# Attention scores on one Trainium2 core: row maxima carried in a spare contraction row of masked queries, instead of in a pass of selector matmuls

## The reference: what is computed

```
patches -> h = patches @ W_embed + b_embed + pos          # 64 images, 196 rows of 256
h = concat(h, txt)                                        # 228 rows per image
q, k, v = LN(h) @ Wq.T, LN(h) @ Wk.T, LN(h) @ Wv.T        # 16 heads of 16
probs = softmax(causal(q k^T / 4));  ctx = probs @ v
h = h + ctx @ Wo.T + bo
h = h + FFN(LN(h))     # ternary weights, RMS norm before each linear, exact gelu, width 1024
```

## Time and profile before

| | us |
|---|---|
| median of 3 runs | 2072.05 (2070.6 to 2072.83) |
| the profiled execution's own time | 2070.54 |
| its span | 2068.8 |
| PE busy | 1939.4 (94%) |
| PE weight loads busy | 1574.5 (76%) |
| VectorE busy | 1514.4 (73%) |
| ScalarE busy | 1296.2 (63%) |
| GpSimd busy | 887.8 (43%) |

### The profile page before, as it was taken

One profiled execution on the slowest core, in us unless ns is written; L12 is line 12 of the kernel. 1 busy time (PEld: TensorE's weight loads), 2 busy tenths in 40 slices (PEclk: granted clock), 3 DMA queues, 4 the chain that ended last, 5 costly groups with the idle time before them and its releaser, 6 DMA issues.

```text
span 2068.8 us, 61840 instructions
## 1 busy us (share of the span) xinstructions
PE 1939.4 (94%) x25986; PEld 1574.5 (76%) x25986; DVE 1514.4 (73%) x2849; ACT 1296.2 (63%) x2050; POOL 887.8 (43%) x1069
## 2 busy tenths in 40 slices
PE   2889999999999999999999999999999999999875
PEld 2668788778778777777877877887787787777664
DVE  5457778778777777777877777787777777777753
ACT  2346666666666666666666666666666666666652
POOL 1124444444444544443444444444444445444443
PEclk8789999999999999999999999999999999999987
DMA  4111111011111101111111111110111111010000
GB/s 133 26 44 40 50 53 49 29 49 40 53 49 53 48 26 49 44 50 52 49 40 39 44 49 49 54 49 28 50 40 53 49 54 46 28 49 22 29 29 23
DMA packets 62989, 93.85 MB, mean 45 GB/s; under 512 B 9634, under 2 KB 59270, under 8 KB 59768
## 3 DMA queue, kind: packets, MB, share of 16 engines
q1 hardware_dynamic: 62712, 89.90, 15.7%
HBM read 45.03 MB, written 14.94 MB: 29 GB/s over the span
## 4 chain that ended last, share of the span: by engine, by line
PE 71%; DVE 20%; issue 4%; ACT 3%; POOL 1%; DMA 1%; DVEq 0%; SPq 0%; POOLq 0%; ACTq 0%
PE dense L327 41%; PE score L327 17%; PE pvps L327 7%; PE dense L384 2%; DVE st L942 2%; DVE rs L914 2%; DVE mx L954 2%; DVE km L990 2%; PE dense L345 2%; DVE h L938 2%; DVE pT_lo L904 2%; PE dense L373 2%; DVE h L1030 1%; DVE mr L966 1%; DVE aT_lo L908 1%
## 5 line engine op out<-in xcount | busy, mean ns | idle before, releaser
L1161 POOL TENSOR_SCALAR_AFFINE_SELECT pr<-pr 114x456 f32<-114x456 f32 x512 | 311.9, 634 | 899.9 <-ACT pr L668 899.9
L668 ACT ACTIVATE pr<-score 114x1368 f32<-114x1368 f32 x256 | 335.7, 1311 | 302.2 <-PE score L327 301.9
L953 DVE TENSOR_REDUCE mx<-score 114x4 f32<-114x456 f32 x256 | 161.4, 630 | 187.3 <-PE score L327 187.1
L954 DVE TENSOR_REDUCE mx<-score 114x4 f32<-114x912 f32 x256 | 281.1, 1098 | 0.0
L327 PE MATMUL dense<-wdn,g 128*114 128x256 bf16 x1024 | 241.0, 281 | 3.5 <-issue 3.5
L1180 POOL TENSOR_TENSOR acc<-acc,sq 128x456 f32<-128x456 f32 x192 | 229.2, 1194 | 18.9 <-POOL acc L1180 0.4
L327 PE MATMUL dense<-wdn,gl 128*114 128x256 bf16 x1024 | 235.1, 275 | 0.0
L327 PE MATMUL score<-km,qs 32*114 32x114 f32 (+1 forms) x4096 | 221.7, 331 | 7.8 <-ACT pr L668 7.6
L327 PE MATMUL pvps<-pr,vp 114*32 114x228 f32 (+1 forms) x4096 | 204.6, 317 | 0.5 <-ACT raw L740 0.5
L914 DVE RECIPROCAL rs<-rs 128x228 f32<-128x228 f32 x128 | 200.8, 1568 | 0.0
L327 PE MATMUL score<-qs,km 32*114 32x228 f32 (+1 forms) x4096 | 196.4, 308 | 0.0
(11 more groups left out here) (135 smaller groups left out, 4423.4 us busy)
## 6 DMA issues: line engine op xcount, KB each, us to landing
pix<-x SPq DMA_DIRECT2D x32, 1176.0 KB
rs<-raw SPq DMA_DIRECT2D x256, 57.0 KB, 2.0
cx<-raw SPq DMA_DIRECT2D x256, 57.0 KB, 2.0
out<-h SPq DMA_DIRECT2D x64, 228.0 KB
h<-txt SPq DMA_DIRECT2D x32, 64.0 KB, 8.0
km<-wqkvo SPq DMA_DIRECT2D x1, 1024.0 KB, 15.4
h<-w_upT SPq DMA_DIRECT2D x1, 1024.0 KB, 14.5
km<-w_embed SPq DMA_DIRECT2D x1, 768.0 KB, 10.3
```

Of the source, the lines that this page charges most:

```text
L668: act(pr[q % 2][:], score[0:R, :, 0:SW], ACT.Exp, scale=float(HD) ** -0.5).then_inc(a["exp"], 1)
L953: nc.vector.tensor_reduce(mx[:, b, 0, :, r], score[0:R, :, 0:R], AX.X, ALU.max)
L954: nc.vector.tensor_reduce(mx[:, b, 1, :, r], score[0:R, :, R:SW], AX.X, ALU.max).then_inc(v["max"], 1)
L1161: nc.gpsimd.affine_select(out=blocks, in_=blocks, compare_op=ALU.is_ge, fill=0.0, base=0, pattern=[[0, 4], [1, R]], channel_multiplier=-1) ...
```

## The change

Each 32-row strip of a score product has 16 rows in which the masked keys were zero. The change keeps a number in one of them. The queries are now copied twice too (`qm`, by `par`), with the other head's rows zeroed; the keys get -1 in one of their 16 spare rows (`minus`), where the masked queries hold 0, so `scores_rows` gives what it gave. When the maxima of an image are known, VectorE adds them to that row of the two query copies (`maxima_in_queries`), and `scores_columns` gives scores minus maxima with no other matmul. VectorE writes the maxima straight into the columns of `mx` that become those rows under a plain f32 transpose; `maxima_rows` is now four f32 transposes and stands in slots 3 and 7. `maxima_parts`, `maxima`, `mT`, `mp` and `sel` are gone.

The values are kept by image: image 1 has two buffers and image 0 one, where there were two for both; `values` computes image 1 first. The rest is order. `DENSE` has its entries elsewhere: `("xt", 1)` is now three behind `("ss", 0)`, and `("mt", 0)` stands ahead of `("emb", 1)`. The first part of the FFN's second product waits for four of the eight low halves of the gelu, where it waited for all. On VectorE, `accl` goes behind the context's `collect`, and the first `context_lo` from slot 5 to slot 6. Constants are built at the very start, the sums of `|w|` in step 1, the ternary weights in steps 1 and 2; the pixel load is in two halves, and `borow` is loaded behind `wqkvo`.

```diff
-DENSE = [("o", 0), ("o", 1), ("pix", 0), ("pix", 1), ("pix", 2), ("mt", 1), ("v", 0), ("pix", 3), ("pix", 4),
+DENSE = [("o", 0), ("o", 1), ("pix", 0), ("pix", 1), ("pix", 2), ("v", 0), ("pix", 3), ("pix", 4),
          ("pix", 5), ("emb", 0), ("x2t", 0), ("x2t", 1), ("up", 0), ("up", 1), ("up", 2), ("up", 3), ("up", 4),
-         ("up", 5), ("up", 6), ("up", 7), ("emb", 1), ("ht", 0), ("ht", 1), ("v", 1), ("mt", 0), ("spare", 0), ("dn", 0),
-         ("dn", 1), ("ss", 0), ("xt", 0), ("xt", 1), ("qk", 0), ("qk", 1), ("qk", 2), ("qk", 3)]
+         ("up", 5), ("up", 6), ("up", 7), ("mt", 0), ("emb", 1), ("ht", 0), ("ht", 1), ("v", 1), ("dn", 0),
+         ("dn", 1), ("ss", 0), ("xt", 0), ("spare", 0), ("xt", 1), ("qk", 0), ("qk", 1), ("qk", 2), ("qk", 3), ("mt", 1)]
 PER = {"pix": 6, "emb": 2, "up": 8, "o": 2, "ht": 2, "xt": 2, "qk": 4, "v": 2, "ss": 1,
        "dn": 2, "x2t": 2, "mt": 2}
...
-        qs = sb("qs", [128, 2, 2, T2], F32)
+        qm = sb("qm", [128, 2, 2, 2, T2], F32)
...
+        spare = sb("spare", [128, 2], F32)
+        minus = sb("minus", [128, 2], F32)
+        vp = sb("vp", [R, 3, 2, H, VW], F32)
+
+        mx = sb("mx", [R, 2, 2, 128], F32)
...
+            load_pixels(0, 0)
             sp.dma_start(stage_e, w_embed).then_inc(s_we, 16)
+            load_pixels(0, 1)
             sp.dma_start(posb[:], pos).then_inc(s_row, 16)
             sp.dma_start(brow, b_embed).then_inc(s_row, 16)
+            sp.dma_start(stage_a, wqkvo).then_inc(s_wa, 16)
             sp.dma_start(borow[:], bo).then_inc(s_row, 16)
-            sp.dma_start(stage_a, wqkvo).then_inc(s_wa, 16)
             sp.dma_start(stage_u, w_upT).then_inc(s_wt, 16)
             for i in range(2):
                 sp.dma_start(stage_d[i], w_downT[:, 1024 * i:1024 * i + 1024]).then_inc(s_wt, 16)
...
+                if blk == 0 and part == 0:
+                    eng.wait_ge(v["gl"], count(5, pair, 2))
+                    eng.wait_ge(p["gl"], count(3, pair, 2))
+                elif blk == 0 and part == 1:
+                    eng.wait_ge(v["gl"], count(5, pair, 5))
...
-                    eng.wait_ge(a["mt"], count(2, pair, b + 1))
+                    eng.wait_ge(v["mq"], count(2, pair, b + 1))
 
                 eng.wait_ge(*score_emptied(t, k, True))
-                for i in range(4):
-                    mm(score[0:R, i, 0:SW], sel[quad(i), r], mT[quad(i), b], start=True, stop=False,
-                       skip_group_check=True)
                 for kb in range(2):
                     c0 = b * S + kb * R
                     for i in range(4):
                         last = mm(score[0:R, i, kb * S:S + kb * R], km[quad(i), buf, m, par, c0:c0 + R],
-                                  qs[quad(i), buf, m, c0:b * S + S], start=False, stop=True,
+                                  qm[quad(i), par, buf, m, c0:b * S + S], start=True, stop=True,
...
             def maxima_rows(pair, b):
 
-                eng.wait_ge(v["m2"], count(2, pair, b + 1))
+                eng.wait_ge(v["max"], count(8, pair, 4 * b + 4))
                 eng.wait_ge(*emptied(pair, "mt", b))
-                for qb in range(2):
-                    last = nc.tensor.transpose(bank_of("mt", b)[:, 0:256].bitcast(BF16)[:, qb * R:qb * R + R],
-                                               mp[:, b, qb].rearrange("p i c -> p (i c)"), identb[0:R, 0:R])
+                for m in range(2):
+                    for qb in range(2):
+                        c0 = m * S + qb * R
+                        last = nc.tensor.transpose(bank_of("mt", b)[:, c0:c0 + R], mx[:, m, qb], ident[0:R, 0:R])
                 last.then_inc(pe["mt"], 1)
...
-                    if Cc and k == 1:
-                        maxima_rows(t - 2, 1)
...
+                    if Bm and k in (3, 7):
+                        maxima_rows(t - 1, k // 4)
...
-                act(qs[:, u, m], bank_of("qk", 2 * m)[:, 0:T2], ACT.Copy).then_inc(a["q"], 1)
+                for par in range(2):
+                    act(qm[:, par, u, m], bank_of("qk", 2 * m)[:, 0:T2], ACT.Copy,
+                        scale=pmask[:, par:par + 1]).then_inc(a["q"], 1)
 
             def odd_keys(pair, u, m):
 
                 eng.wait_ge(v["km"], count(2, pair, m + 1))
-                act(km[:, u, m, 1], bank_of("qk", 2 * m + 1)[:, 0:T2], ACT.Copy,
-                    scale=pmask[:, 1:2]).then_inc(a["km"], 1)
+                act(km[:, u, m, 1], bank_of("qk", 2 * m + 1)[:, 0:T2], ACT.Identity,
+                    bias=minus[:, 0:1], scale=pmask[:, 1:2]).then_inc(a["km"], 1)
...
-                ps = bank_of("mt", b)[:, 0:256].bitcast(BF16)
-                act(mT[:, b, 0:S], ps[:, 0:S], ACT.Copy)
-                act(mT[:, b, S:SW], ps[:, R:S], ACT.Copy).then_inc(a["mt"], 1)
...
+                m, par = divmod(r, 2)
                 eng.wait_ge(pe["s"], count(8, pair, k + 1))
-                if k % 4 == 0 and began(pair - 1):
-                    eng.wait_ge(v["m2"], count(2, pair - 1, b + 1))
-                nc.vector.tensor_reduce(mx[:, b, 0, :, r], score[0:R, :, 0:R], AX.X, ALU.max)
-                nc.vector.tensor_reduce(mx[:, b, 1, :, r], score[0:R, :, R:SW], AX.X,
+                if k == 0 and began(pair - 1):
+                    eng.wait_ge(pe["mt"], count(2, pair - 1, 2))
+                elif k == 4:
+                    eng.wait_ge(pe["mt"], count(2, pair, 1))
+                x = 16 * (1 - par)
+                nc.vector.tensor_reduce(mx[:, m, 0, x:128:32], score[0:R, :, 0:R], AX.X, ALU.max)
+                nc.vector.tensor_reduce(mx[:, m, 1, x:128:32], score[0:R, :, R:SW], AX.X,
                                         ALU.max).then_inc(v["max"], 1)
...
+            def maxima_in_queries(pair, buf, b):
+
+                eng.wait_ge(pe["mt"], count(2, pair, b + 1))
+                for par in range(2):
+                    w = qm[:, par, buf, :, b * S:b * S + S]
+                    last = nc.vector.scalar_tensor_tensor(
+                        out=w, in0=bank_of("mt", b)[:, 0:T2].rearrange("p (m s) -> p m s", m=2),
+                        scalar=spare[:, 1 - par:2 - par], in1=w, op0=ALU.mult, op1=ALU.add)
+                last.then_inc(v["mq"], 1)
...
-                ts(km[:, u, m, 0], bank_of("qk", 2 * m + 1)[:, 0:T2], pmask[:, 0:1], None,
-                   ALU.mult).then_inc(v["km"], 1)
+                ts(km[:, u, m, 0], bank_of("qk", 2 * m + 1)[:, 0:T2], pmask[:, 0:1], minus[:, 1:2],
+                   ALU.mult, ALU.add).then_inc(v["km"], 1)
...
+                    if t == 0 and k == 3:
                         weights_rest()
-                        absolute_sums()
-                    if isinstance(t, int) and t == 0 and k == 5:
-                        ternary()
+                    if Cc and k == 0:
+                        maxima_in_queries(t - 2, u, 1)
                     if Bm:
                         maxima_unit(t - 1, k)
-                    if Bm and k == 3:
-                        maxima_parts(t - 1, 0)
+                    if t == 1 and k in (1, 2, 3):
+                        absolute_sum(k - 1)
+                    if t == 1 and k == 5:
+                        ternary_bounds()
+                    if t == 1 and k == 6:
+                        ternary(0)
+                    if t == 2 and k in (2, 4):
+                        ternary(k // 2)
...
-                    if Bm and k == 7:
-                        maxima_parts(t - 1, 1)
```

221 lines of the change are left out of this document (94 added, 127 removed).

## The result

| | before | after |
|---|---|---|
| median, us (range, runs) | 2072.44 (2070.6 to 2073.46, 4) | 2038.53 (2038.08 to 2038.7, 4) |
| profiled span, us | 2068.8 | 2037.0 |
| matmuls | 25986 | 25090 |
| VectorE busy, us (instructions) | 1514.4 (2849) | 1467.2 (2717) |

Ratio 0.9837, 95% interval 0.9822 to 0.9853. The changed kernel is 34 us faster, where the forecast had 62 (2010 us, range 1992 to 2032): the direction is right, the size about half, and the time is outside the range. The profiled execution took 2038.7 us, 1.7 more than its span.

What follows compares the result with a forecast made beforehand. TensorE was taken as the bound, busy 59.68 of 60.83 us a step. Full steps 50.5, start 10, steps 1 and 2 -1.5, end 2.8 sum to 61.8 us less: 2010 us as a median, range 1992 to 2032.

Steps and rivals of the forecast that it cites:

- The selector pass: TensorE, ahead of the column scores: each dropped group of four takes 0.19 us off the stream, 1.52 us a step.
- Rival 2: A selector group costs its whole 0.36 us, so a step loses 1.4 us more: 1971 us; chance 0.05.
- The transposes of the maxima: TensorE: two groups of four f32 transposes take 0.88 us a step where 0.60 was spent: 0.28 more.
- The waits: TensorE: the 0.58 us ahead of the second `xt` transposes goes, about 0.45 remains ahead of the query product; 0.5 gained.
- Two large operations for each image: VectorE, slots 0, 3 and 4: 1.35 us an image (bounds 1.0 to 2.3), costing nothing under TensorE's cover.
- Rival 3: The pair of large VectorE operations is late and holds the bank ring: 2045 us at 2.3 a pair; chance 0.06.
- Nothing in a full step: Values by image, half pixel loads, down product's weaker wait, `accl` and context order: no cost in a full step.
- rival 1: The chain over VectorE and ScalarE sets slots 7 to 1, so 1.2 us a step comes off: 2026; chance 0.15.
- Start and steps 1 and 2: Start: net 10 us gained, after 2 us against it for the later `borow`; steps 1 and 2: net 1.5 us lost.
- End: Steps 32 to 34: 1.2 us from 13 units, about 1.6 from `collect` filling the wait of `accl`; 2.8 us gained.

## Why the prediction was wrong

- **"The selector pass": 0.19 us each. This is the step that failed.** The distance from pass to scores was read rightly (0.19), but taken as the whole of what the stream would save. It is what the stream saves *ahead of* the scores; behind that point the scores grow by 0.10, since their first loads no longer run beside the pass (first four products 0.443 us each, 0.348 behind a pass). Net 0.09: 8 x 0.10 x 29 = 23 of the 28 us that are missing. The claim that failed is that products with unchanged shapes keep their cost when their neighbour goes. Rival 2 erred further on the wrong side, and no rival had the cost below 0.19.
- **"The transposes of the maxima": 0.28.** Measured 0.31. Right.
- **"The waits": 0.50 gained.** 0.56 in the changed kernel, 0.58 alone. The waits that end and remain were named rightly; that the sum fits so well is luck, as two errors cancel. The stretch of the `xt` transposes gave 0.77 and not 0.58, and the one ahead of the query product grew by 0.21 and not by 0.08 (a gap of 0.45 was to remain; it is 0.58 in its row). The wait in slot 1, at the place that the maxima's transposes left, gave 0.08 more, which the sum didn't have.
- **"Two large operations for each image": nothing.** They take 675 to 694 ns, where 0.675 was reckoned, near the key copy. All 128 of them, with their times (min/median/max ns):

```profile
L954 DVE SCALAR_TENSOR_TENSOR qm<-dense,spare,qm x128: 675/682/694, 71.6 to 1952.3; 128x456 f32<-128x456 f32 x128
```

  The column scores of slot 0 don't wait for them, nor do the embedding transposes of slot 4. Rival 3 is out. (Of the small operations that went, two and not one have both inputs in SBUF, `mr<-mx,mp` and `mp<-mr,mp`; no term hung on it.)
- **"Nothing in a full step" for all else.** 0.2 us a step of small growth, 6 us in all, which I didn't list. 0.09 is the up product behind its low halves in slot 2. 0.07 is in slot 6, where the `xt` transposes now start only when VectorE has ended the first half of `final` (748.25 + 0.88 = 749.13); before, that half ended 0.50 us ahead of them. VectorE, then TensorE:

```profile
748.25 0.88 DVE L1016 SCALAR_TENSOR_TENSOR h<-dense,ssq,h 114x256 f32<-114x256 f32 x2
```

```profile
749.27 0.97 PE L381 MATMUL dense<-ident,xn 114*128 114x114 f32 x8
```

  The last 0.03, in slot 4, is no wait: the first down product takes 0.16 to the next behind the value products, and took 0.13 behind the maxima's transposes. So it is a mild form of rival 1: the chain over VectorE does come in, but at slots 2 and 6, where TensorE came later before and so waited less (slot 2, 0.08) or not at all (slot 6).
- **Start and steps 1 and 2: 8.5.** 6.1 came. The start itself was right to 0.2 us; the loss is in step 1, 4.2 us, where I had reckoned with a net 1.5. I had counted the reductions ahead of the transposes of slot 3 (that wait is 1.75 us) but not the absolute sum of slot 1, although the diff puts it ahead of the low halves there.
- **End: 2.8.** 1.6 came. `accl` to the second norm is 11.63 us where it was 12.45, 0.8 for the 1.6 reckoned (VectorE):

```profile
1985.92 0.63 DVE L1113 TENSOR_TENSOR accl<-acc 128x456 f16<-128x456 f32 x1 [1.07 <-POOL acc L1168]
...
1997.55 1.40 DVE L930 BATCH_NORM_STATS2 st<-h 114x6 f32<-114x256 f32 x4
```

- **The range** was made for errors in the waits and in VectorE's operations. The largest term of the sum, 44 us, had its lower bound at its own value. That term alone at 0.09 would have given 2033.

## What to carry to other kernels

When a short pass goes, ask what had been loading behind it: price it as the difference of two block lengths, with and without, and if the trace has only one of them, bound the gain from below by the pass less the load that ran beside it (here 0.19 - 0.17 = 0.02 to 0.19, and 0.09 came). When the bounding engine gets faster, go through each place where it takes an input and compare the input's end with the new arrival; a wait of zero with 0.1 us of slack is a wait to come. And look at waits on "all parts" and at the bank ring before touching arithmetic: one place in a list (19.5 us) and one wait taken apart (15 us) each gave more here than the whole rewrite of the maxima (12 us).

## What the runs showed of the hardware

- A block of 16 float32 products over 32 rows (4 beside each other, 114 weight columns) spans 0.85 to 0.86 us behind a product over 128 rows, and 0.75 behind a bf16 pass over 32 rows. The difference is in the first four products (0.443 and 0.348 us). Its order of widths makes no difference (0.78 and 0.79; 0.68 and 0.67).
- A weight load is early behind a product of its own kind (128 rows behind 128: 966.18, with the product's start; 32 behind 32: 906.16) and late where the kind changes (966.66, 967.44).
- What stands *behind* such a block counts too: a bf16 pass over 32 rows starts 0.68 us after the block's start, the float32 value products over 114 rows 0.78, with the same span of the block.
- Eight float32 transposes in one piece take 0.88 to 0.90 us to the next product, but 1.67 when a wait of 0.58 cuts them in two: 0.2 us more than the wait that the row shows.
- A scalar-times-tensor-plus-tensor operation on VectorE over 128 x 456 float32, one input in PSUM and one in SBUF, takes 0.682 us, with 3% between shortest and longest of 128.
